# Spreading the value matmuls of an attention chain: one k tile every four steps instead of two every eight

## The reference

```python
qkv = einsum('oc,bchw->bohw', w_qkv, norm(x))           # q, k, v of 8 heads
attn = softmax(einsum('bhdi,bhdj->bhij', q * scale, k)) # 1024 x 1024 for each head
y = einsum('bhij,bhdj->bhdi', attn, v)
x = x + w_proj @ y                                      # layer 0: + position bias, then a layer norm
```

## Time and profile before

| what | value |
|---|---|
| median of 3 runs | 510.47 us (510.2 to 511.23) |
| the profiled execution | 510.87 us, its span 509.1 us |
| granted TensorE clock over the span | 0.978 of full |
| PE, DVE, ACT, POOL busy | 94%, 67%, 54%, 43% |
| steps of layer 0 | 32.3 to 135 us |
| steps of layer 1 | 193.9 to 308 us |
| steps of layer 2 | 354.4 to 468 us |

### The profile page before, as it was taken

The page is one execution under the profiler, slowest core; times in us unless marked ns, Lnnn a source line. Parts: engine busy times, 40 slices in busy tenths (PEclk is TensorE's granted clock), DMA queues, the critical chain, the costliest instruction groups (busy, mean ns, idle before and its releaser), DMA issues.

```text
span 509.1 us, 7000 instructions
## 1 busy us (share of the span) xinstructions
PE 478.5 (94%) x2264; PEld 240.1 (47%) x2264; DVE 340.6 (67%) x645; ACT 272.5 (54%) x520; POOL 217.6 (43%) x203
## 2 busy tenths in 40 slices
PE   8799999999899999999999989999999999989996
PEld 6444444443239565444444322664544444432463
DVE  7599888883264468987867522738988776722573
ACT  3228777777423324876757761131777765764032
POOL 8300031101000003899879981000699789987000
PEclk9979999999997999999999999998999999999999
DMA  5330442101000154488864540034457865452002
GB/s 146 55 56 22 136 67 35 21 5 21 1 0 1 26 116 106 86 197 172 185 118 88 94 91 6 1 91 105 93 115 155 178 120 102 84 102 46 0 1 82
DMA packets 18795, 39.85 MB, mean 78 GB/s; under 512 B 6478, under 2 KB 7638, under 8 KB 18632
## 3 DMA queue, kind: packets, MB, share of 16 engines
q1 hardware_dynamic: 13464, 23.39, 19.8%
q0 software_dynamic: 5152, 16.00, 17.1%
q10 hardware_dynamic: 144, 0.02, 0.0%
HBM read 4.76 MB, written 1.05 MB: 11 GB/s over the span
## 4 chain that ended last, share of the span: by engine, by line
PE 68%; DVE 10%; DMA 5%; SPq 4%; issue 4%; ACT 4%; POOL 3%; ACTq 0%; POOLq 0%; DVEq 0%
PE S L935 15%; PE PV L973 14%; PE S L962 13%; DVE max L705 6%; PE S L1083 4%; DMA k_stack<-kL 4%; POOL SUMS L492 3%; PE M L989 3%; PE PV L890 2%; SPq L301 2%; ACT E L556 2%; PE S L916 2%; PE M L916 2%; PE PV L916 2%; SPq L308 2%
## 5 line engine op out<-in xcount | busy, mean ns | idle before, releaser
L705 DVE TENSOR_REDUCE max<-S 128x1 f32<-128x512 f32 x384 | 239.0, 674 | 21.0 <-PE S L935 20.8
L556 ACT ACTIVATE E<-S 128x512 f32<-128x512 f32 x384 | 212.7, 604 | 71.5 <-PE S L962 67.3
L492 POOL TENSOR_TENSOR SUMS<-E 128x512 f32<-128x512 f32 x126 | 165.7, 1446 | 122.1 <-ACT E L556 122.0
L935 PE MATMUL S<-k_stack,q_stack 126*128 126x512 f32 x384 | 182.0, 484 | 9.4 <-DVE max L705 4.2
L962 PE MATMUL S<-q_stack,k_stack 128*128 128x512 f32 x384 | 155.3, 414 | 4.7 <-DMA q_stack<-mHL 2.3
L935 PEld LDWEIGHTS S<-k_stack,q_stack 126*128 126x128 f32 x384 | 74.0, 193 | 85.2 <-DVE max L705 60.2
L973 PE MATMUL PV<-E,V 128*32 128x512 f32 x768 | 95.4, 599 | 1.7 <-ACT pv_sb L563 1.7
L962 PEld LDWEIGHTS S<-q_stack,k_stack 128*128 128x128 f32 x384 | 72.5, 191 | 37.3 <-ACT E L556 22.1
L718 DVE TENSOR_TENSOR mHL<-S,mHL 4x128 fp32r<-4x128 f32 x48 | 13.3, 278 | 45.6 <-ACT mHL L545 45.6
L545 ACT ACTIVATE mHL<-S 4x128 fp32r<-4x128 f32 x48 | 12.6, 262 | 56.4 <-PE S L953 56.4
L973 PEld LDWEIGHTS PV<-E,V 128*32 128x32 f32 x768 | 20.0, 109 | 44.7 <-issue 26.9
(11 more groups left out here) (181 smaller groups left out, 334.4 us busy)
## 6 DMA issues: line engine op xcount, KB each, us to landing
SUMS<-SUMS POOLq DMA_DIRECT2D x30, 512.0 KB, 6.3
k_stack<-kH SPq DMA_DIRECT2D x32, 128.0 KB, 2.5
q_stack<-qH SPq DMA_DIRECT2D x40, 64.0 KB, 2.0
k_stack<-kL SPq DMA_DIRECT2D x16, 128.0 KB, 3.3
q_stack<-qH SPq DMA_DIRECT2D x16, 128.0 KB, 2.3
q_stack<-mHL SPq DMA_DIRECT2D x96, 2.0 KB
rec_sb<-den_sb SPq DMA_DIRECT2D x6, 256.0 KB
q_stack<-qL SPq DMA_DIRECT2D x20, 64.0 KB, 2.0
```

The costliest lines, as they stand in the source:

```text
L492: pool.tensor_tensor(SUMS[:, slot, :], E[:, E_PLAN[s][0], :], E[:, E_PLAN[s + 1][0], :], ALU.add).then_inc(sum_ready, 1)
L556: act.activation(E[:, slot, :], B[:, ring_of_scores(s) % B_RING, :], ACT.Exp, scale=1.0 if l == 0 else float(HEAD_DIM[l]) ** -0.5).then_in ...
L705: dve.tensor_reduce(max8[:, m % 2, r:r + 1], A[:, n % A_RING, :], AX.X, ALU.max, negate=True).then_inc(a_used, 1)
L935: pe.matmul(A[:, n % A_RING, :], q_stack[0:SHIFT_ROW, slot, q0:q0 + P], k_stack[0:SHIFT_ROW, slot, k0:k0 + HALF], start=True, stop=True).t ...
```

## The change

The value matmuls of blocks 0 to 2 were issued two key tiles at a time, at steps 29, 37, 45, 53 of a block (counted from the block's first step). Now one tile is issued at each of the steps 27, 31, 35, 39, 43, 47, 51, 55. The two denominator groups of these blocks stood together at step 49; now the first stands behind the value tile of step 47 and the second behind that of step 51. The shift rows of units 3 to 15 (PE's transpose, ACT's and DVE's copies and SP's two DMAs) are placed 8 steps ahead of their unit, where they were 10 ahead. The last block, the counts of instructions and the semaphores stay as they were.

```diff
-SUMS_STEP = 29
-DEN_STEP = 49
+VALUE_STEP = 27
+VALUE_GAP = 4
+DEN_TILES = (5, 6)
...
 def rows_step(j):
-    return TILES * j - (10 if j > 2 else 6)
+    return TILES * j - (8 if j > 2 else 6)
...
-                    b, k, phase = (s - SUMS_STEP) // 32, (s - SUMS_STEP) % 32 // 8, (s - SUMS_STEP) % 8
-                    if 0 <= b < BLOCKS - 1:
-                        if phase == 0:
-                            values(l, b, 2 * k)
-                            values(l, b, 2 * k + 1)
-                    if l and s >= DEN_STEP and (s - DEN_STEP) % 32 == 0:
-                        denominators(l, (s - DEN_STEP) // 32, 0)
-                        denominators(l, (s - DEN_STEP) // 32, 1)
+                    b, t, phase = (s - VALUE_STEP) // 32, (s - VALUE_STEP) % 32 // VALUE_GAP, (s - VALUE_STEP) % VALUE_GAP
+                    if 0 <= b < BLOCKS - 1 and phase == 0:
+                        values(l, b, t)
+                        if l and t in DEN_TILES:
+                            denominators(l, b, DEN_TILES.index(t))
```

## The result

The change made the kernel slower: 522.9 us median (518.26 to 524.75, 4 runs) against 510.85 us (510.2 to 512.83, 4 runs) for the kernel before, a ratio of 1.0216 with a 95% interval of 1.0142 to 1.0289. The forecast was 506.2 us in a range of 500 to 510.8, so both its sign and its range were wrong. The profiled execution took 522.35 us.

The account below looks back on a forecast made before the run. DVE sets the pace, with value matmuls adding ring waits; in layers 1 and 2 SP's loads and POOL stand close. Gains of 2.3 + 2 x 1.0 = 4.3 us from 510.87 give 506.6, median 506.2; range 500 to 510.8.

Parts of the forecast that it names:

- Part 1: One value tile every four steps on PE: a unit of eight steps takes 6.17 us, gain 0.30, bounds 0 to 0.60.
- The doubled overhead: On PE, a burst of one value tile costs 1.00 us to the next S, so two cost 2.0, not 1.85.
- The sum: PE's time per unit: a group of four steps is 3.07 us, a unit with its transpose 6.17.
- Part 2: Next block's first tile at step 59 waits for ACT's copy of PV: 0.6 us, twice a layer, 1.2 us.
- Part 3: Denominators at steps 47 and 51, layers 1 and 2: 0.93 us each, together the 1.85 of before; nothing counted.
- the bound: POOL's reuse of SUMS slots may hold one add for about 1 us per block; bounds 0 and 1.0.
- Part 4: Shift rows two steps later: S doesn't wait, but loads of heads 5 to 7 start 0.94 us later against the steps.
- Some 2 us of landing make 4: Shift rows take 1.84 us to SP's next instruction plus some 2 landing, against 6.17 of eight steps: no wait.
- the 1.84 us to SP: Time from PE's transpose through ACT's copy, DVE's subtraction and two SP DMAs to SP's next instruction.
- 24.0 us of chain, the same: Layers 1 and 2, first load issue to last landing, needed at step 68: 24.0 us, unchanged.
- POOL's 6.2 sets the pace: Last units of layers 1 and 2: POOL's 6.2 us replaces 6.47 as the pace, gain 0.25 us.
- The rival with the right sign: Slower by the load chain in layers 1 and 2: grows from 24.0 to 27.2 us, total 512.6; chance 0.13.

Follow-up runs that it names:

- run 1: The changed kernel with the shift rows of units 3 to 15 back at ten steps ahead, value tiles and denominators still spread: 514.67 us, ratio 1.0084.
- Run 9: The changed kernel with the shift rows of units 6, 7 and 8 alone at ten steps ahead: 512.28 us, ratio 1.0035.
- run 13: The changed kernel with block 0's folding DMA ahead of head 7's load in layers 1 and 2, rows still eight steps ahead: 518.5 us, ratio 1.0154.
- Run 4: The changed kernel with value tiles from step 29, denominators at 49 and 53, and shift rows ten steps ahead: 504.12 us, ratio 0.9890.
- Run 10: The changed kernel with the shift rows of unit 4 alone at ten steps ahead: 520.66 us, ratio 1.0172.
- Run 11: The changed kernel with the shift rows of unit 14 alone at ten steps ahead: 517.43 us, ratio 1.0118.
- Run 5: The changed kernel with the shift-row DMAs of units 3 to 15 issued from ACT's queue instead of SP's: 536.61 us, ratio 1.0468.

## Why the prediction was wrong

**Part 1, values every four steps: right in kind, the gain a third smaller than forecast.** The pace went from 6.45 to 6.26, 0.19 and not 0.30. DVE's idle time ahead of L719 fell to 0.65 us, as the prediction had it (from 1.18 to about 0.6). The doubled overhead appeared in mid stream: a tile takes 1.00 us to the next matmul. The sum was 0.10 short, since the four steps behind a transpose take 3.20 us (82.76 to 85.96 in layer 0) and only the next four the 3.07 that was forecast for both. What the part left out is that the 0.33 us for the transpose hold only behind a tile. In the changed kernel it does stand there, so the sum wasn't hurt; run 1 shows that in mid stream the transpose would have taken the whole gain.

The clock was 1.00 in the ten units before, and 1.00 in the changed kernel with half the batch, in the window shown above. The rule of the Trainium skill (Perfetto Trace Analysis, Matmul Optimizations), that matmuls be issued back to back in batches because power is scaled with use, did not price this edit: in those units the split batches lost no clock. The clock fell where PE had waited. The changed kernel has the granted clock at 0.50 in four new stretches of some 3.4 us (layer 1 from 259.4 and 303.8, layer 2 from 423.2 and 471.0). Two of them follow PE's waits of 2.20 us in layer 1 and 2.17 us in layer 2; the other two follow waits of S of step 120 for its rows, 1.03 and 2.31 us. A wait alone doesn't settle it: the kernel before waited 1.00 us for those rows in layer 1 and kept its clock. Run 9, with steps 64 to 72 at 6.28 us, had none in the steps of these two layers. The price of one stretch can be read. Steps 72 to 80 of layer 1 hold the first of them and no wait of PE, and took 8.64 us; in layer 2 they took 7.11 at full clock, and in layer 1 of run 13 they took 7.09. That is 1.5 us. Four such stretches would be 6 us; this is an estimate, and an upper one, since PE is not always the limit at the end of a layer.

**Part 2, the first tile at step 59: right, and cheaper.** The two units took 6.63 instead of 6.27, 0.36 us where 0.6 was taken. Run 4 with the tile at step 61 has 6.27 there.

**Part 3, the denominators: next to nothing, as said.** PE waits for SUMS only at a layer's end. The two groups cost 1.7 us a block (7.09 + 7.13 less two units of 6.26), where they had cost 1.5 (7.99 less 6.45). POOL's add at step 51 was held for 1.00 us, as the bound had it; no run shows that this cost anything.

**Part 4, the rows: the step that failed.** Its first half was right. The load of a head starts 1.50 to 1.59 us behind S in layer 0, where 1.49 was forecast. Three sentences behind it were not, and they are the failed step: the price of everything in SP's queue behind the late rows was put at nothing.

- *"Some 2 us of landing make 4, against 6.17 of eight steps: S of the unit doesn't wait."* The landing was 4.2 us for unit 5 and 5.6 for unit 9. In both cases SP had just issued a stack load, and an accumulating DMA of POOL was in flight too (issued at 223.06 and 250.84), at unit 9 also the weight load; no run separates them. And the 1.84 us to SP hold only where SP is free. Rows of unit 5 stand behind head 4's load, which itself stands behind the rows of unit 4. The prediction looked at the loads of heads 5 to 7 alone. Run 10 shows this wait going with unit 4 alone. Steps 32 to 40 had lost 1.3 and 0.9 us in the two layers.
- *"Then 24.0 us of chain, the same."* Up to the landing that step 68 waits for, this was nearly so: from the first load at 228.54 to 253.15 there are 24.6 us in layer 1. But the chain was taken to end there. The fold, the weight load and the rows of unit 9 stand behind it in SP's queue, and the sum never moved them. They left 2.1 to 3.2 us later against the layer's start, more than the load's own delay, and had no slack: DVE's longest wait for the fold grew from 0.6 to 3.87 us, and S of step 72 waited 2.2. Steps 64 to 80 lost 4.0 and 4.8 us in the two layers. Run 9 brings 10.6 us back with the rows ahead of the three loads alone, run 13 brings 7.5 back with the fold alone.
- *"In the last units POOL's 6.2 sets the pace instead of 6.47: 0.25."* The spread of reciprocals, behind the rows of unit 14, left 0.95 us later against S of step 104, landed 1.4 us more slowly, and POOL's product waited 4.43 us. Steps 104 to 127 lost 2.3 and 2.5 us. Run 11 gives 5.5 us back by the medians with unit 14 alone.

The rival with the right sign had the right place, the loads behind the rows, and part of the mechanism. It needed a chain to step 68 that was 2.2 us longer or more, by the fourth accumulating DMA, and its mark was the wait of step 68. The chain grew by 0.6 us, begun 1.0 us later against the layer's start (36.0 us behind S of step 0, where it was 35.1), and that wait fell from 1.23 to 0.80 us, in the main because step 40 had already stood for 1.3 us. An accumulating DMA did come up against head 7's load, the third and not the fourth, and what grew with it was the time that SP was held, by 2.7 us, and so the delay of all that SP issues next. The sum of the rival counted the landing and not the order behind it, so its chance of 0.13 was low.

Run 5 takes the rows from SP's track and loses 14 us more: rows from ACT's queue waited 4.5 us beside a DMA that SP had issued at the same time. The Trainium skill (DMA: Bandwidth & Descriptors, Issuing engines are not separate DMA queues) says that DMAs of all issuing engines run on the same 16 DMA engines and interleave; that wait agrees with it.

**Open.** How much of the 12 us is the lower clock is known for one stretch only. The share of the weight load at step 72 of layer 1 was not separated, and what holds SP in head 7's load was not tested: a run with POOL's accumulating DMA held until that load is issued would do it. The single parts add to more than the whole, and the runs don't say how they combine.

## What to carry to other kernels

Before a step that issues DMAs is moved in an in-order queue, list everything queued behind it down to the layer's end, with the slack of each. The delay is paid where there is none, and that need not be the transfer that is first in line. The unit that is seen waiting is not the one to move: here undoing units 5, 9 and 15 gave nothing and undoing 4, 6, 7, 8 and 14 gave all. Two edits that meet on one engine have to be priced together: spreading the value tiles is worth 1.1% when the transpose keeps its place behind a tile and the rows stay early, and costs 0.8% or 2.2% otherwise.

## What the runs showed of the hardware

- Two DMAs of 2 KB issued behind a stack load of layer 1, with an accumulating DMA of POOL in flight, took 4.2 and 5.6 us to land.
- SP needed 3.1 to 3.4 us to issue a load of six DMAs when POOL's accumulating DMA of 512 KB came 1.4 us or more behind the load's first DMA, and 5.0 to 6.1 us when it came with it or ahead of it (36 loads of head 7 in 18 profiles, one of them between, at 4.2 us). The cause was not tested.
- The DMA that spreads the reciprocals (its outer dimension is 4) took 9.6 us from issue to use before the change (285.84 to 295.44) and 11.0 us after (289.51 to 300.49). Small DMAs issued at its time from another engine waited for 4.5 us.
- A transpose in float32 between S and maximum matmuls costs 0.22 to 0.27 us per unit more than one right behind a value tile.
- Waits cost twice. After PE had stood for 2.20 and 2.17 us at steps 68 to 72 the granted clock was 0.50 for a stretch, with value tiles of 1.52 and 1.94 us instead of 1.06. One such stretch cost 1.5 us.
